# A graph layer over 100,000 rows: row centring by bfloat16 products, and the degree masks made on ScalarE

## The reference

```python
deg = maximum(segment_sum(ones(dst.shape), dst, num_segments=100000), 1.0)
norm = deg ** -0.5
h = maximum(layernorm(x), 0.0)                  # per row, no gain or bias
msg = h[src] @ W1 + h[src] * h[dst] @ W2
msg = msg * (norm[src] * norm[dst])
y = segment_sum(msg, dst, num_segments=100000) + h @ W1
y = where(y >= 0, y, 0.2 * y)
y = y / maximum(sqrt(sum(y * y, axis=1)), 1e-12)
out = x + y
```

## Time and profile before

| | us |
|---|---|
| median of 3 runs (lowest, highest) | 928.2 (927.44, 931.21) |
| the profiled execution's own time | 928.79 |
| its span | 927.1 |

### The profile page before, as it was taken

How to read it: one execution, slowest core, us unless ns; L and a number is a source line. 1 busy time by engine, 2 the same in 40 slices (tenths; PEclk the granted TensorE clock), 3 DMA queues, 4 the chain that set the end, 5 groups by cost and what they waited for, 6 DMA issues and landing times.

```text
span 927.1 us, 21508 instructions
## 1 busy us (share of the span) xinstructions
PE 734.7 (79%) x6104; PEld 713.7 (77%) x6104; DVE 870.1 (94%) x2878; ACT 711.0 (77%) x2944; POOL 682.0 (74%) x694
## 2 busy tenths in 40 slices
PE   1499888888987988888878898798798887988820
PEld 1398878888887987888877888798788887988810
DVE  6789999999999999999999999999999999999980
ACT  0079887797887987887879788797888888779950
POOL 1777888888788788787788887888888887833472
PEclk9999998898998998998989899898999999889965
DMA  2813746646645655755754664675665665653532
GB/s 71 304 50 90 242 155 196 232 162 201 237 163 197 238 173 188 241 181 180 234 201 164 209 236 165 207 239 165 207 238 168 200 247 166 210 201 131 172 138 60
DMA packets 68804, 172.90 MB, mean 186 GB/s; under 512 B 14383, under 2 KB 34514, under 8 KB 62434
## 3 DMA queue, kind: packets, MB, share of 16 engines
q1 hardware_dynamic: 49868, 135.41, 43.1%
q0 software_dynamic: 18816, 36.08, 12.7%
HBM read 96.89 MB, written 77.04 MB: 188 GB/s over the span
## 4 chain that ended last, share of the span: by engine, by line
DVE 79%; issue 10%; PE 3%; ACT 3%; DMA 1%; DVEq 1%; POOL 0%; SPq 0%; POOLq 0%; ACTq 0%
DVE bst L784 20%; DVE xo L829 19%; DVE ybuf L837 10%; DVE cjk L753 7%; DVE agg L859 5%; DVE oe L821 5%; DVE ye L942 3%; DVE ge L745 2%; DVE ge L746 2%; ACT junk L973 1%; DMA xin<-in_x 1%; PE pt L1106 1%; DVE scs L876 1%; DVE rd L907 1%; DVE d L765 1%
## 5 line engine op out<-in xcount | busy, mean ns | idle before, releaser
L1106 PE MATMUL pt<-nident,bst 128*128 128x128 f32 x1568 | 300.5, 296 | 0.0
L467 POOL DMA_INDIRECT out<-oe,sstage x196 | 234.7, 1198 | 60.3 <-issue 59.1
L1106 PEld LDWEIGHTS pt<-nident,bst 128*128 128x128 f32 x1568 | 265.0, 212 | 0.0
L462 POOL DMA_INDIRECT xs<-in_x,stage x196 | 215.5, 1099 | 53.3 <-issue 52.7
L462 POOL DMA_INDIRECT xd<-in_x,stage x196 | 208.8, 1065 | 59.7 <-issue 59.7
L1116 PE MATMUL pu<-w,ct 128*128 128x128 f32 x1568 | 222.5, 293 | 22.4 <-ACT ct L957 22.4
L1103 PE MATMUL pt<-ident,xin 128*128 128x128 f32 x784 | 230.8, 294 | 7.9 <-DVE bst L784 4.8
L973 ACT ACTIVATE junk<-ybuf 128x128 bf16<-128x128 f32 x784 | 233.3, 306 | 0.7 <-DVE ybuf L837 0.7
L829 DVE SCALAR_TENSOR_TENSOR xo<-ybuf,rd,xin 128x128 f32<-128x128 f32 x784 | 226.6, 341 | 0.0
L1116 PEld LDWEIGHTS pu<-w,ct 128*128 128x128 f32 x1568 | 202.3, 205 | 29.4 <-ACT ct L957 25.8
L957 ACT ACTIVATE ct<-pt 128x512 f32<-128x512 f32 x196 | 116.3, 593 | 55.1 <-PE pt L1106 53.9
(11 more groups left out here) (136 smaller groups left out, 1165.2 us busy)
## 6 DMA issues: line engine op xcount, KB each, us to landing
xin<-in_x SPq DMA_DIRECT2D x96, 512.0 KB, 4.5
out<-xo SPq DMA_DIRECT2D x48, 1024.0 KB
srow<-src_rows SPq DMA_DIRECT2D x49, 256.0 KB, 6.9
edge_rows<-oe SPq DMA_DIRECT2D x49, 256.0 KB
same<-same_segment SPq DMA_DIRECT2D x49, 128.0 KB, 6.2
xs<-in_x,stage POOLq DMA_INDIRECT x196, 2.9
xd<-in_x,stage POOLq DMA_INDIRECT x196, 3.7
out<-oe,sstage POOLq DMA_INDIRECT x196
```

The source lines that it names most:

```text
L462: pool.indirect_dma_start(out=to, out_offset=None, in_=rows, in_offset=bass.IndirectOffsetOnAxis(ap=index, axis=0), bounds_check=limit, oo ...
L467: pool.indirect_dma_start(out=out, out_offset=bass.IndirectOffsetOnAxis(ap=index, axis=0), in_=rows, in_offset=None, bounds_check=row_limi ...
L1106: last = pe.matmul(pt[:, q % 2, f], mean[:, s.buf(0, 2), col:col + 1].to_broadcast([P, D]), nident[:], start=False, stop=True)
```

## The change

The two masks of the lookup become two signs, computed by ScalarE from `srow` with a per-partition bias (`edge`, which holds one half more and one half less than `-first`). A sum of the two signs, with halved table entries, stands for the masks; so `fcar` gets two columns and the last lookup products double from four to eight. The row means are no longer read as float32 by TensorE. The DVE forms two remainders by two subtractions (`mean_rest`), so that the mean lies as three bfloat16 parts in place; TensorE turns all 48 columns by one product (`turn_means`), ScalarE copies the result to `mt` (`copy_means`), and each block is centred by one bfloat16 product of `mt` and a broadcast column of `pickb`. The signs stand in ScalarE's step after `copy_quarter(0)`. TensorE's step now waits for the loaded rows and for `mt`, not for the statistics.

```diff
+        parts = [bst[:, h, 0:TD * 3].bitcast(BF16)[:, 1::2] for h in range(2)]
+        upper = bst[:, :, 0:TD * 3].rearrange("p b (t w) -> p b w t", w=3)
         mean = bst[:, :, 1::3]
...
+            dve.tensor_scalar(edge[:, 0:1], first[:], -1.0, 0.5, ALU.mult, ALU.add)
+            dve.tensor_scalar(edge[:, 1:2], first[:], -1.0, -0.5, ALU.mult, ALU.add).then_inc(s_first, 1)
...
-            dve.tensor_scalar(ftab[:, 0, :], fdp[:, 0, :], 32.0, None, ALU.mult)
-            dve.tensor_scalar(ftab[:, 1, :], fdp[:, 1, :], 0.25, None, ALU.mult).then_inc(s_ftab, 1)
+            dve.tensor_scalar(ftab[:, 0, :], fdp[:, 0, :], 16.0, None, ALU.mult)
+            dve.tensor_scalar(ftab[:, 1, :], fdp[:, 1, :], 0.125, None, ALU.mult).then_inc(s_ftab, 1)
...
-            def row_masks(s, d, i=None):
-                h = s.buf(d, 2)
-                dve.wait_ge(srow_loaded[s.buf(d)], s.dma(d))
-                if i is None or i + d >= 2:
-                    dve.wait_ge(lk_done, s(d - 1) * 2)
-                dve.tensor_scalar(ge[:, h, 0, :], srow[:, s.buf(d), :], first[:, 0:1], None, ALU.is_ge)
-                dve.tensor_scalar(ge[:, h, 1, :], srow[:, s.buf(d), :], first[:, 0:1], None, ALU.is_equal
-                                  ).then_inc(ge_done, 1)
...
-            for d in range(2):
-                row_masks(Step(0, 0), d, 0)
...
-            row_masks(Step(0, 0), 2, 0)
...
+            def mean_rest(s, d, k):
+                b = s.buf(d, 2)
+                dve.wait_ge(bn_done, s(d + 1))
+                if k:
+                    dve.wait_ge(rest_done, s(d + 1))
+                word, to = ((mean[:, b, 0:TD], upper[:, b, 0, :]), (upper[:, b, 0, :], upper[:, b, 2, :]))[k]
+                high = bst[:, b, 0:TD * 3].bitcast(BF16)[:, (3 if k == 0 else 1)::6]
+                dve.tensor_tensor(to, word, high, ALU.subtract).then_inc((rest_done, parts_done)[k], 1)
             def out_edges(s, first, last):
...
                                       ).then_inc(d2_ready, 1)
...
-                        dve.wait_ge(t_done, s() * NQ)
+                        dve.wait_ge(mt_done, s())
                     stats_dense(s, 1, 0, 4, i)
...
                     stats_guard(s, 1)
+                    mean_rest(s, 1, 0)
...
                         stats_edges(s, 1, k)
+                        if k == 0:
+                            mean_rest(s, 1, 1)
...
                     out_dense(s, 13, TD)
-                if has(i, 3):
-                    row_masks(s, 3)
...
+            def row_signs(s, d, i=None):
+                h = s.buf(d, 2)
+                act.wait_ge(srow_loaded[s.buf(d)], s.dma(d))
+                if i is None or i + d >= 2:
+                    act.wait_ge(lk_done, s(d - 1) * 2)
+                for sign in range(2):
+                    last = act.activation(ge[:, h, sign, :], srow[:, s.buf(d), :], ACT.Sign, bias=edge[:, sign:sign + 1])
+                last.then_inc(ge_done, 1)
+            act.wait_ge(s_first, 1)
+            for d in range(3):
+                row_signs(Step(0, 0), d, 0)
+            def copy_means(s, d):
+                act.wait_ge(mt_done, s(d + 1))
+                act.copy(mt[:], pe_m[0:3 * TD, 0:P]).then_inc(mt_evac, 1)
...
             act.activation(dd[:], d2[:], ACT.Sqrt).then_inc(dd_ready, 1)
+            copy_means(Step(0, 0), 0)
...
                     copy_quarter(0)
+                if has(i, 3):
+                    row_signs(s, 3, i)
...
                     b = s.buf(-2)
...
                     copy_quarter(3)
+                if has(i, 1):
+                    copy_means(s, 1)
...
                     squares(-1, 5, 10)
...
                 if half:
...
-                        last = pe.matmul(pe_x[:, 2 * RW + k:2 * RW + k + 1], ge[:, h, 1, k * P:(k + 1) * P], fcar[:],
-                                         start=True, stop=True)
+                        for sign in range(2):
+                            last = pe.matmul(pe_x[:, 2 * RW + k:2 * RW + k + 1], ge[:, h, sign, k * P:(k + 1) * P],
+                                             fcar[:, sign:sign + 1], start=sign == 0, stop=sign == 1)
...
+            def turn_means(s, d):
+                pe.wait_ge(parts_done, s(d + 1))
+                pe.matmul(pe_m[0:3 * TD, 0:P], parts[s.buf(d, 2)], identb[:], start=True, stop=True).then_inc(mt_done, 1)
...
+            turn_means(Step(0, 0), 0)
...
                                   is_transpose=True, start=True, stop=False)
-                        last = pe.matmul(pt[:, q % 2, f], mean[:, s.buf(0, 2), col:col + 1].to_broadcast([P, D]),
-                                         nident[:], start=False, stop=True)
+                        if q == 0 and t == 0:
+                            pe.wait_ge(mt_evac, s(1))
+                        last = pe.matmul(pt[:, q % 2, f], pickb[:, col:col + 1].to_broadcast([3 * TD, P]), mt[:], start=False, stop=True)
...
-                    pe.wait_ge(bn_done, s(1))
+                    pe.wait_ge(x_loaded[s.buf()], s.dma() + more(i, 0))
+                    pe.wait_ge(x_loaded2[s.buf()], s.dma() + more(i, 0))
                     turn_quarter(0)
...
                     mul_quarter(3)
+                if has(i, 1):
+                    if has(i, -1):
+                        pe.wait_ge(msg_done, s())
+                    turn_means(s, 1)
+                if has(i, 0):
                     h = s.buf(0, 2)
```

More of the change, by code:

```diff
@@ L99, in gnn_preln_kernel @@
         ident = sb("ident", [P, P])
-        nident = sb("nident", [P, P])
+        identb = sb("identb", [P, P], BF16)
+        pick = sb("pick", [3 * TD, TD])
+        pickb = sb("pickb", [3 * TD, TD], BF16)
+        mt = sb("mt", [3 * TD, P], BF16)
         w1 = sb("w1", [P, D])
@@ L116, in gnn_preln_kernel @@
         ftab = sb("ftab", [P, 2, RW], F16)
-        fcar = sb("fcar", [P, 1], F16)
+        fcar = sb("fcar", [P, 2], F16)
+        edge = sb("edge", [P, 2])
         fcarf = sb("fcarf", [P, 1])
@@ L204, in gnn_preln_kernel @@
         s_const = sem("s_const")
+        s_pick = sem("s_pick")
         s_ch = sem("s_ch")
@@ L220, in gnn_preln_kernel @@
         s_ftab = sem("s_ftab")
+        s_first = sem("s_first")
         s_flag = sem("s_flag")
@@ L267, in gnn_preln_kernel @@
         ye_done = sem("ye_done")
+        rest_done = sem("rest_done")
+        parts_done = sem("parts_done")
+        mt_done = sem("mt_done")
+        mt_evac = sem("mt_evac")
         t_done = sem("t_done")
@@ L585, in _ @@
             dve.wait_ge(s_ident, 1)
-            dve.tensor_scalar(nident[:], ident[:], -1.0, None, ALU.mult).then_inc(s_const, 1)
+            thirds = ident[0:3 * TD, 0:3 * TD].rearrange("p (t w) -> p t w", w=3)
+            dve.tensor_reduce(pick[:], thirds, AX.X, ALU.add, negate=True).then_inc(s_const, 1)
             dve.wait_ge(s_nat, 16 * (6 + 3 * len(whole(QF))))
@@ L727, in _ @@
             chain(dve.memset(first[0:1, :], -1.0))
[L728 removed]
+            dve.tensor_scalar(edge[:, 0:1], first[:], -1.0, 0.5, ALU.mult, ALU.add)
+            dve.tensor_scalar(edge[:, 1:2], first[:], -1.0, -0.5, ALU.mult, ALU.add).then_inc(s_first, 1)
+            chain(dve.tensor_scalar(cjk[:, 0, :], fdp[:, 1, :], first[:, 0:1], None, ALU.is_equal, ALU.add, accum_out=fcarf[:]))
+            dve.tensor_scalar(fcar[:, 0:1], fcarf[:], 0.5, None, ALU.mult)
+            dve.tensor_scalar(fcar[:, 1:2], fcarf[:], -0.5, None, ALU.mult)
+            chain(dve.tensor_scalar(fdp[0:1, 1, :], fdp[0:1, 1, :], -1, None, ALU.mult))
             chain(dve.tensor_tensor(fdd, fdp[:, 0, :], fdp[:, 1, :], ALU.subtract))
[L730 removed]
             dve.tensor_scalar(fdp[:, 0, :], fdd, 7, None, ALU.logical_shift_right)
             chain(dve.tensor_scalar(fdp[:, 1, :], fdd, 127, None, ALU.bitwise_and))
[L733 to L734 removed]
+            dve.tensor_scalar(ftab[:, 0, :], fdp[:, 0, :], 16.0, None, ALU.mult)
+            dve.tensor_scalar(ftab[:, 1, :], fdp[:, 1, :], 0.125, None, ALU.mult).then_inc(s_ftab, 1)
             ndf = nd[:].rearrange("p q h -> p (q h)")
             s4f = s4[:].rearrange("p q h -> p (q h)")
[L739 to L747 removed]
             def count_one(s, d, half, k):
@@ L844, in _ @@
             stats_guard(Step(0, 0), 0)
+            for k in range(2):
+                mean_rest(Step(0, 0), 0, k)
             def do(s, i):
@@ L948, in _ @@
         def _(act):
+            act.wait_ge(s_const, 1)
+            act.copy(identb[:], ident[:])
+            act.copy(pickb[:], pick[:]).then_inc(s_pick, 1)
+            def row_signs(s, d, i=None):
[12 more added lines that the diff above has]
+                act.copy(mt[:], pe_m[0:3 * TD, 0:P]).then_inc(mt_evac, 1)
             act.wait_ge(dg_done, 1)
             act.activation(dd[:], d2[:], ACT.Sqrt).then_inc(dd_ready, 1)
+            copy_means(Step(0, 0), 0)
             def do(s, i):
```

12 lines of the change are left out of this document (8 added, 4 removed).

## The result

| | kernel before | changed kernel |
|---|---|---|
| median | 929.42 us (927.44 to 932.08, 20 executions) | 924.01 us (915.95 to 940.04, 20 executions) |
| changed / before | | 0.9923, 95% interval 0.9903 to 0.9943 |
| profiled execution (its span) | 928.8 us (927.1) | 915.95 us (914.2) |

The change gains 0.8%, some 7 us of the 21.9 that were forecast (5.4 us between the medians above), and 906.5 us with its range of 897 to 918 was wrong. Three of the changed kernel's executions (929.83, 931.98 and 940.04 us) ran in a slower state and are left out of the ratio; the median of the other 17 is 922.8 us. The profiled execution is the quickest of the twenty, 8 us under the median, so the trace shows the gain at its best.

What follows compares the result with a forecast made beforehand. The DVE was taken to bound the kernel. From the profiled 928.8 us, -34.0 + 8.1 + 4 + 2 - 2 = -21.9 gave 906.9, stated as 906.5 us, range 897 to 918.

Steps and rivals of the forecast that it cites:

- TensorE gets lighter: TensorE's centring of rows: transposes with bfloat16 products spare 2.7 us a step, price 0 in the middle.
- Two subtractions: DVE's two added 16-column subtractions for the means: 0.09 us each over 45 steps, +8.1 us (+4 to +17).
- The masks leave the DVE: DVE's mask pair in each step is dropped: 0.79 us in 43 steps, -34.0 us.
- The row loads come nearer: Loads before the next step's row statistics have less room to land: +4 us (0 to +20).
- "ScalarE", price 0: ScalarE's step: two signs and a copy add 1.35 us, covered by its waits, so price 0.
- The start: Steps 0 and 1, where the DVE waits for TensorE and ScalarE: -2 us (-4 to +1).
- the drift against GpSimd: DVE and GpSimd transfers disturb each other as their phase wanders: +2 us (0 to +8).
- B: Row load becomes the wait of most steps, 0.4 us a step instead of 0.1: 919.5 us; chance 0.08.
- C: GpSimd, never idle in the middle, becomes the bound: 912 us, at most all the gain lost; chance 0.07.
- D: TensorE, idle longer, gets a lower clock and sets a longer step: 989 us at 0.58; chance 0.04.
- E: ScalarE's signs need another function table, two loads a step: 979 us, or 1103 by the skill; chance 0.01.
- F: GpSimd transfers hold up DVE's two subtractions, 0.9 us each: +81, 987.5 us; chance 0.01.

Runs made afterwards that it cites:

- the padded kernel: The changed kernel with the picking matrix and copied means padded with zero rows from 48 to 128; 903.4 us, ratio 0.9718 to the kernel before.
- the signs alone: The changed kernel with the mean part taken back to float32 products, masks still ScalarE signs; 905.5 us, ratio 0.9734 to the kernel before.

## Why the prediction was wrong

**The step that failed: "TensorE gets lighter".** It took 0.055 us for the product from a product with 128 rows and carried it over to one of 48 rows between transposes of 128. With 128 rows the estimate is right: 0.16 to 0.17 us a pair against 0.155. With 48, each pair costs 0.25 us more, 16 x 0.25 = 4.0 us a step: instead of sparing 2.7 us it added 16 x 0.09 = 1.4. "Price 0 in the middle" rested on TensorE idling ahead of the product of the parts. It did so for 27.8 us in 28 waits, and for 92.1 in 44 when padded.

What that did to the time, against the padded kernel: 6.0 us at the start (103.20 against 97.18 us), and 8.5 us in the 43 steps. Of the latter, 7.2 lie in three steps of 19.44, 18.35 and 20.50 us that are 16.63, 17.34 and 17.15 in the padded kernel; the last is the stretch from 460 us shown above. Between the profiled executions this makes 914.2 - 899.6 = 14.6 us. The medians lie 922.8 - 903.4 = 19.4 apart, and the 17 executions of the changed kernel that the ratio counts spread over 11.6 us (915.95 to 927.55) where the padded one's five lie within 3. That the other 5 us are more such stretches at the low clock is likely, since only TensorE's load differs, but it is not shown: the changed kernel has one trace.

**"Two subtractions", +8.1 forecast, too dear.** The first is free: from the reciprocal to `oe` it is 518.23 - 517.88 = 0.35 us, as in the earlier trace rows without it, since `oe` waits for the reciprocal anyway (the cheap bound named this). The second costs 0.08. Against the kernel with the signs alone the short steps are 0.03 us longer, so the term is 1.4 to 3.6 us (45 steps of 0.03 or 0.08).

**"The masks leave the DVE", -34.0,** nearly right: the short steps fall from 17.33 to 16.60 with the signs alone, 0.73 x 43 = -31.

**"The row loads come nearer", +4,** right in size for the changed kernel (2.8 us in 5 waits) and for the signs alone (5.1 us in 8), too much for the padded one (0.4 us):

```profile
DVE bst L792 <- DMA xin<-in_x: 2.8, 5, 0.9
```

**"ScalarE", price 0,** right: 1.39 us a step for 1.35, and VectorE waited for it 2.7 us in all. As foretold, TensorE's wait for the masks is gone, and ScalarE waits for `ye` only 1.0 us in all. **The start, -2,** wrong in sign for the changed kernel (+6.0) and 0 for the padded one: the first centring came 1.95 us later (44.10 against 42.15) where about 1 us had been allowed, and even a short pair only makes up for that.

The padded kernel took 901.3 us in its profiled execution against the forecast's 906.9. That nearness is in part luck, for the errors are larger than their sum: the subtractions and the row loads were 8 to 10 us too dear, and the masks 3 and the start 2 us too hopeful. For the term of +2, the drift against GpSimd, no run shows a value.

**The rivals.** B did not come (2.8 us, not 17). C did not: GpSimd kept pace at 16.63 us a step. D had the right engine and the wrong reason. It asked whether TensorE would be left too idle; it became too full, at a clock of 0.94 in the middle, and nothing was left to cover a stretch at the low level. E and F did not come: the step of 16.74 us has room for neither a table load nor a held-up subtraction. F would have made the two subtractions dear, and the trace shows 0.16 to 0.17 us for each, as for L892 before.

## What to carry to other kernels

Before pricing a small TensorE product, look at its neighbours: at full clock a product of 48 rows between products of 128 cost more than the float32 product with twice the passes that it replaced. Pad it with zero rows, which cost nothing measurable here, or put the small ones side by side. And an engine that is busy for 85% of the time is not free of price because the chain leaves it out: read its pitch at the start, at full clock and at the low level, and see what is left of its idle time in each before calling it covered.

## What was not expected of the hardware

- Each change between 128 and 48 rows costs 0.09 to 0.13 us at full clock in bfloat16, and (0.67 - 0.33) / 2 = 0.17 in float32; between 128 and 96 rows it costs nothing measurable. At the low level the pair with 48 rows takes 0.62 us and the padded one 0.32.
- A 16-column subtraction between the reciprocal and its first reader is free on VectorE (0.35 us from one to the other with it and without).
- Leaving the 16 mean products out altogether (904.4 us) is no faster than having them with 128 rows (903.4 us).
- The two parts of the change do not simply add: by the ratios -25 us and +23 us alone, -7 together, 5 us better than their sum.
